# Attention of a two-layer gated network on one core: bank rotation, order of the query and key preparation, and two steps moved to GpSimd

## The chip, the cores and the metric

One Trainium2 chip, one of its cores. The metric is the device time of one execution in microseconds (us), lower is better. Names of engines: PE is TensorE, DVE is VectorE, ACT is ScalarE, POOL is GpSimd, SP is SyncE.

## The reference

Sixteen sequences ("batches") of 256 rows by 256 features go through four residual steps. Two of them matter here only as neighbours.

```
x += tanh(g_xattn[0]) * retention(layernorm(x), ctx)       # layer 0, decayed running sum
x += tanh(g_ffn[0])   * fp4_swiglu(layernorm(x))           # layer 0, 4-bit block quantised
x += tanh(g_xattn[1]) * attention(layernorm(x), ctx, ctx)  # layer 1, 16 heads of 16
x += tanh(g_ffn[1])   * bfp_mlp(layernorm(x))              # layer 1, block floating point
# attention: q = rope(q), k = rope(k); softmax(q k^T / 4 + alibi bias) v
```

All of it is float32 to the outside. x and ctx stay in SBUF from the first load to the last store.

## The kernel before, in words

The program of each engine is written out by hand; engines meet at counting semaphores. There are three stages over the 16 batches: layer 0, attention, and the MLP, and each engine's program runs a body per batch in each stage, with some work of neighbouring batches in it. The attention stage is the one that changes.

**Preparation of a batch (two bodies ahead).** DVE takes the layer-norm statistics of x (`at_qk_a`, L1477 to L1483), POOL raises the variance to the power -1/2 (`at_rstd`, L1178), DVE normalises (`at_qk_norm`, L1489 and L1492), POOL multiplies with the cosine and the sine table (`at_k_parts` L1173 and L1174, `at_q_parts` L1183 and L1184), DVE adds the two products (`at_rope`, L1501) and writes a rounded high part twice into a stack (`at_high_part`, L1513), POOL writes the rest as a low part (`at_low_part`, L1166). The stack holds q and k of all heads with bias rows, so that a product of two rounded matrices gives full precision.

**A body b of PE (`at_body`).** It transposes the stack of batch b+1 in eight groups of four (`at_turn`, L579), each into a 512-wide bank, and ACT copies each to SBUF (`at_turned`, L934). In between it transposes the row maxima of batch b (`at_turn_max`, L606), which ACT negates (`at_max_out`, L955) and SP places as two extra rows of the transposed stack with two DMAs (`at_place_max`, L398), and it transposes the output of batch b-1 (`at_turn_out`, L643). Then come, interleaved, sixteen groups m of score products of batch b+1 that serve only to find the row maxima (`at_scores_for_max`, L599; DVE reduces each with `at_row_max`, L1523), sixteen groups u of scores of batch b, already less their maximum (`at_scores`, L620; ACT takes the exponential of each, `at_exponent`, L943), and eight groups of products with the values (`at_times_v`, L635; ACT copies four results, `at_pv_out`, L949). Two groups u are issued among the transposes, and one after each m but 7 and 15.

**Banks.** PSUM has eight in the stage. Two (`a_ps_t`) take the transposed groups in turn, two (`a_ps_m`) take maxima groups, two the scores, two the values' product. From m = 4 on the maxima groups use `a_ps_t` and `a_ps_m` by pairs, so that four are in rotation; m = 2 and 3 reuse the banks of m = 0 and 1. The transposed maxima go into the first bank of `a_ps_m`.

**Body b of DVE:** statistics of b+2, rope and high part of k of b+2, norm of b+2, output of b-1 (`at_add_attention`: two reciprocals L1530, two products L1534, gate times result plus x at L1537), then the sixteen maxima of b+1, with rope of q after m = 5 and its high part after m = 8. **Body b of POOL:** k parts, rstd, low part of k, q parts, low part of q of b+2. ACT copies the values into a padded array after u = 8 (`at_v_of`, L926). Before the first body a prologue prepares the first two batches, interleaved with the end of layer 0, and finds the maxima of the first.

In the last but one body DVE and POOL round the MLP's weights, in the last PE transposes them.

Of the kernel before, what the change touches and what calls it, by code (L numbers as in the profile page):

```python
# [12 lines left out]
ALU = mybir.AluOpType  # L13
# [3 lines left out]
P = 128  # L17
# [107 lines left out]
V_QK = ["stats0", "stats1", "aggr0", "aggr1", "var", "rope_k", "k_hi", "rstd4", "norm0", "norm1", "rope_q", "q_hi"]  # L125
V_QK_FIRST = ["stats0", "stats1", "aggr0", "aggr1", "var", "rope_k", "rstd4", "norm0", "norm1", "k_hi", "rope_q", "q_hi"]
G_QK = ["k_cos", "k_sin", "rstd", "k_lo", "q_cos", "q_sin", "q_lo"]
G_QK_FIRST = ["k_cos", "k_sin", "rstd", "q_cos", "q_sin", "k_lo", "q_lo"]
V_OUT = ["recip0", "recip1", "share0", "share1", "add"]
# [14 lines left out]
LAST_IN_TURN_BANKS = 6  # L144


def build_main(nc, load, loaded, out_v, g_xattn, g_ffn, w_gate_up, w_down, w_fc, b_fc, w_proj, b_proj, ident, decay,
# [3 lines left out]
    with ExitStack() as keep:  # L151
# [146 lines left out]
        def group_in_same_max_bank(m):  # L298
            return m - 4 if m >= 6 else m - 2
# [44 lines left out]
        a_v_qk, a_g_qk, a_v_max, a_v_out = sem("v_qk"), sem("g_qk"), sem("v_max"), sem("a_v_out")  # L344
# [3 lines left out]
        a_alone = sem("a_waits_alone")  # L348
        f_v_ln, f_g_rstd, f_v_shift, f_a_norm = sem("f_v_ln"), sem("f_rstd_ready"), sem("f_shift_ready"), sem("f_normed")
# [13 lines left out]

        def v_qk_steps(b):
            return V_QK if b.shifted(-1) else V_QK_FIRST

        def g_qk_steps(b):
            return G_QK if b.shifted(-1) else G_QK_FIRST
# [57 lines left out]
        def _(pe):  # L426
# [220 lines left out]
            def at_body(b):  # L647
# [153 lines left out]
        def _(act):  # L801
# [119 lines left out]
            def at_v_of(b):  # L921
                if b.shifted(-2):
                    act.wait_ge(a_t_pv, b.shifted(-2).count(PG, PG))
                elif b.i == 0:
                    act.wait_ge(a_v_aug_laid, 1)
                nc.scalar.copy(a_v_aug[:, b.par, :, :, 0:HD].rearrange("p c h d -> p (c h) d"),  # L926
                               tiles(ctx, b).rearrange("p c (h d) -> p (c h) d", d=HD)).then_inc(a_v, 1)

            def at_turned(b, g):
                act.wait_ge(a_t_t, b.count(TG, g + 1))  # L930
                if g == 0 and b.shifted(-2):
# [3 lines left out]
                               a_ps_t[:, g % 2, :]).then_inc(a_t, 1)  # L935
# [21 lines left out]
            def at_body(b):  # L957
# [14 lines left out]
                for u in range(2, SU):  # L972
# [3 lines left out]
                    if u == 8 and nxt:  # L976
                        at_v_of(nxt)
# [80 lines left out]
            at_v_of(first)  # L1058
# [17 lines left out]
        def _(pool):  # L1076
# [84 lines left out]
            def at_low_part(b, which):  # L1161

                pool.wait_ge(a_v_qk, upto(v_qk_steps(b), b, ("q_hi", "k_hi")[which]))
# [3 lines left out]
                                        s[:, :, 0:HD], ALU.subtract).then_inc(a_g_qk, 1)  # L1167

            def at_k_parts(b):
# [3 lines left out]
                nc.gpsimd.tensor_tensor(a_part_cos[:, 1, :], kb, a_cos[:, :], ALU.mult).then_inc(a_g_qk, 1)  # L1173
                nc.gpsimd.tensor_tensor(a_part_sin[:, 1, :], kb, a_sin[:, :], ALU.mult).then_inc(a_g_qk, 1)  # L1174

            def at_rstd(b):
                pool.wait_ge(a_v_qk, upto(v_qk_steps(b), b, "var"))
                nc.gpsimd.tensor_tensor(a_rstd[:, b.par], a_var[:, b.par], neg_half[:, :], ALU.pow).then_inc(a_g_qk, 1)  # L1178

            def at_q_parts(b):  # L1180
                qb = a_qn[:, :, :].rearrange("p c d -> p (c d)")
                pool.wait_ge(a_v_qk, upto(v_qk_steps(b), b, "norm1"))
                nc.gpsimd.tensor_tensor(a_part_cos[:, 0, :], qb, a_cos[:, :], ALU.mult).then_inc(a_g_qk, 1)  # L1183
                nc.gpsimd.tensor_tensor(a_part_sin[:, 0, :], qb, a_sin[:, :], ALU.mult).then_inc(a_g_qk, 1)  # L1184
# [586 lines left out]
```

## Time and profile before

| what | value |
|---|---|
| median of 3 runs | 830.58 us (827.97 to 831.57) |
| profiled execution, its own time | 830.41 us |
| profiled execution, span | 828.3 us |
| PE, DVE, ACT, POOL busy over the span | 85%, 83%, 59%, 52% |
| attention bodies | from about 363 to 669 us |

The span runs from the first to the last instruction of the trace; the time of the execution holds 2.11 us more around it. In the timeline a row is: start in us, length in us, engine, line, operation, tiles, count, and in brackets how long the engine sat idle before it and what ended that. PEld is the weight load of a matmul. Rows merge neighbouring instructions; the ends of matmuls are modelled, so the distance between two starts tells more than a length.

### The profile page before, as it was taken

What the parts mean: (1) busy time and instruction counts of PE and PEld (TensorE: products, weight loads), DVE (VectorE), ACT (ScalarE), POOL (GpSimd) and SP (SyncE); (2) the same over time, 40 slices, a digit from 0 to 9 for tenths busy, and PEclk for the clock granted to TensorE, in tenths of its full rate; (3) what the DMA queues carried; (4) which work ended last, traced back from release to release, by engine and by line L of the source; (5) the groups of instructions that cost most, each with busy time, mean ns of one, the idle gap of its engine ahead of it and who ended that gap; (6) DMA issues with size and microseconds to landing.
All of it is one profiled execution on the core that took longest, in us unless ns stands there. A gap on an engine that the chain in (4) does not pass through costs nothing.

```text
span 828.3 us, 16569 instructions
## 1 busy us (share of the span) xinstructions
PE 706.1 (85%) x5090; PEld 516.6 (62%) x5090; DVE 689.9 (83%) x1230; ACT 485.8 (59%) x955; POOL 430.8 (52%) x331
## 2 busy tenths in 40 slices
PE   2365999999999998689999999999999867767775
PEld 1254888888888876566666666666665424444443
DVE  6856888888888788878999999899998558888885
ACT  3333445555445342338887788887887755555653
POOL 3523656555665655744445555544454426555553
PEclk9676999999999999889999999999999797898899
DMA  8710000000000000010000000000001000000011
GB/s 275 239 34 0 1 1 1 0 0 0 0 0 1 1 1 1 1 51 3 3 2 2 1 1 2 1 1 1 1 1 52 2 1 13 26 26 25 27 39 51
DMA packets 17719, 18.35 MB, mean 22 GB/s; under 512 B 1670, under 2 KB 16912, under 8 KB 17680
## 3 DMA queue, kind: packets, MB, share of 16 engines
q1 hardware_dynamic: 17084, 17.66, 6.6%
q8 instruction: 21, 0.34, 0.2%
q10 hardware_dynamic: 596, 0.20, 0.1%
q14 instruction: 18, 0.15, 0.1%
HBM read 13.39 MB, written 4.19 MB: 21 GB/s over the span
## 4 chain that ended last, share of the span: by engine, by line
PE 58%; DVE 18%; issue 9%; ACT 8%; POOL 4%; DMA 1%; POOLq 0%; DVEq 0%; ACTq 0%; SPq 0%
PE ps_o L540 9%; PE a_ps_pv L635 7%; PE a_ps_t L579 7%; PE a_ps_s L620 6%; PE a_ps_m L599 5%; DVE f_ps_small L1608 4%; PE ps_gu L504 4%; PE ps_gu L506 4%; PE ps_gu L505 4%; PE a_ps_t L599 3%; DVE f_hcode L1624 2%; DVE maxima L1523 2%; PE a_ps_pv L643 1%; ACT stack_t L934 1%; ACT probs L943 1%
## 5 line engine op out<-in xcount | busy, mean ns | idle before, releaser
L943 ACT ACTIVATE probs<-a_ps_s 128x512 f32<-128x512 f32 x256 | 148.1, 602 | 30.3 <-PE a_ps_s L620 25.7
L1523 DVE TENSOR_REDUCE maxima<-a_ps_m 128x2 f32<-128x512 f32 x160 | 102.6, 682 | 11.1 <-PE a_ps_m L599 11.0
L620 PE MATMUL a_ps_s<-stack_t 64*128 64x256 f32 x512 | 102.6, 315 | 3.1 <-ACT probs L943 1.5
L540 PE MATMUL ps_o<-w2t,hqt 128*128 128x256 f32 (+1 forms) x384 | 99.1, 393 | 1.3 <-ACT hqt L871 0.7
L1166 POOL TENSOR_TENSOR stack<-roped,stack 128x512 f32<-128x512 f32 x32 | 42.8, 1337 | 109.6 <-DVE stack L1513 108.2
L504 PE MATMUL ps_gu<-w1h,yth 128*128 128x352 f32 x256 | 86.8, 339 | 4.6 <-DVE h L1336 4.6
L934 ACT CAST stack_t<-a_ps_t 128x512 fp32r<-128x512 f32 x128 | 71.8, 584 | 31.1 <-PE a_ps_t L579 30.8
L635 PE MATMUL a_ps_pv<-probs,v_aug 128*32 128x256 f32 x1024 | 84.9, 404 | 3.0 <-ACT probs L943 2.9
L579 PE MATMUL a_ps_t<-idf,stack 128*128 128x128 f32 x512 | 76.8, 290 | 8.8 <-POOL stack L1166 5.1
L505 PE MATMUL ps_gu<-w1l,yth 128*128 128x352 f32 x256 | 83.1, 325 | 0.0
L506 PE MATMUL ps_gu<-w1h,ytl 128*128 128x352 f32 x256 | 83.1, 324 | 0.0
L540 PEld LDWEIGHTS ps_o<-w2t,hqt 128*128 128x128 f32 (+1 forms) x384 | 66.3, 189 | 22.1 <-issue 12.4
L620 PEld LDWEIGHTS a_ps_s<-stack_t 64*128 64x128 f32 x512 | 68.2, 191 | 16.4 <-ACT probs L943 8.9
L579 PEld LDWEIGHTS a_ps_t<-idf,stack 128*128 128x128 f32 x512 | 57.8, 146 | 25.6 <-ACT stack_t L934 8.8
L1523 DVE TENSOR_REDUCE maxima<-a_ps_t 128x2 f32<-128x512 f32 x96 | 62.9, 681 | 11.2 <-PE a_ps_t L599 11.2
L1140 POOL TENSOR_TENSOR hq<-hcode,hscale 128x1408 f32<-128x1408 bf16 x16 | 41.5, 2592 | 56.5 <-DVE hcode L1355 56.5
L599 PE MATMUL a_ps_m<-stack_t 64*128 64x256 f32 x320 | 66.1, 322 | 3.8 <-DVE maxima L1523 2.9
L863 ACT ACTIVATE sg<-ps_gu 128x352 f32<-128x352 f32 x64 | 29.6, 463 | 67.5 <-PE ps_gu L506 67.5
L599 PEld LDWEIGHTS a_ps_m<-stack_t 64*128 64x128 f32 x320 | 43.1, 187 | 34.3 <-DVE maxima L1523 18.8
L1215 POOL TENSOR_TENSOR f_hup<-f_h,f_hmag 128x2048 f32<-128x2048 f32 x16 | 58.3, 3641 | 10.5 <-DVE f_hcode L1624 9.5
L1005 ACT ACTIVATE f_h<-f_ps_fc 128x512 f32<-128x512 f32 x64 | 36.1, 597 | 36.4 <-POOL f_hup L1215 36.2
L1336 DVE TENSOR_TENSOR h<-sg,ps_gu 128x352 f32<-128x352 f32 x64 | 33.2, 518 | 28.2 <-ACT sg L863 27.9
(181 smaller groups left out, 1703.9 us busy)
## 6 DMA issues: line engine op xcount, KB each, us to landing
xres<-in_x SPq DMA_DIRECT2D x16, 256.0 KB, 3.2
ctx<-in_ctx SPq DMA_DIRECT2D x16, 256.0 KB, 3.8
out_x<-f_y SPq DMA_DIRECT2D x16, 256.0 KB, 2.1
w1a_raw<-in_w_gate_up SPq DMA_DIRECT2D x1, 1024.0 KB, 5.8
w_raw<-in_w_fc SPq DMA_DIRECT2D x1, 1024.0 KB, 5.5
w_raw<-in_w_proj SPq DMA_DIRECT2D x1, 1024.0 KB, 4.9
w_raw<-in_w_down SPq DMA_DIRECT2D x1, 704.0 KB, 9.2
stack_t<-neg_max_t SPq DMA_DIRECT2D x32, 8.0 KB
```

What stands on the lines that cost most here:

```text
L504: nc.tensor.matmul(into, yth[:, kc, c, :], w1h[:, kc, cols], start=kc == 0, stop=False)
L505: nc.tensor.matmul(into, yth[:, kc, c, :], w1l[:, kc, cols], start=False, stop=False)
L506: ins = nc.tensor.matmul(into, ytl[:, kc, c, :], w1h[:, kc, cols], start=False, stop=kc == KD - 1)
L540: ins = nc.tensor.matmul(ps_o[:, c, :], hqt[0:rows, g, n, :], w2t[0:rows, k, :], start=k == 0, stop=k == KH0 - 1)
L579: ins = nc.tensor.transpose(a_ps_t[:, g % 2, (n * C + c) * P:(n * C + c + 1) * P], a_stack[:, b.par, which, c, 2 * pair:2 * pair + 2, :].r ...
L599: ins = nc.tensor.matmul(max_bank(m)[:, n, :], a_stack_t[b.par][rows, 0, pair, c * P:(c + 1) * P], a_stack_t[b.par][rows, 1, pair, :], sta ...
L620: ins = nc.tensor.matmul(a_ps_s[:, half, n, :], a_stack_t[b.par][rows, 1, pair, kc * P:(kc + 1) * P], a_stack_t[b.par][rows, 0, pair, :], ...
L635: ins = nc.tensor.matmul(a_ps_pv[32 * n:32 * n + 32, quad % 2, 0:T], a_v_aug[:, b.par, kc, 4 * quad + n, :], a_probs[:, (2 * g + n % 2) % ...
L934: nc.scalar.copy(a_stack_t[b.par][:, g % 2, pair:pair + 2, :].rearrange("p a t -> p (a t)"), a_ps_t[:, g % 2, :]).then_inc(a_t, 1)
L943: nc.scalar.activation(a_probs[:, u % 8], a_ps_s[:, u % 2], ACT.Exp).then_inc(a_exp, 1)
L1215: nc.gpsimd.tensor_tensor(f_blocks(f_hup[:, :]), f_blocks(f_h[:, b.par]), f_spread(f_hmag[:, b.par], F_NBH), ALU.add).then_inc(f_g_hup, 1)
L1523: nc.vector.tensor_reduce(a_maxima[:, b.par, c, 4 * quad + half:4 * quad + half + 3:2], max_bank(m), X, ALU.max).then_inc(a_v_max, 1)
```

## The change

Transposed groups g and maxima groups m both rotate over the four banks of `a_ps_t` and `a_ps_m`, by pairs. Scores u follow every m up to 13. Statistics of batch b+4 and the norm of b+3 are taken in body b, rope and high parts of k and q of b+2 at its start, and nothing but maxima after m = 0. POOL multiplies the values by the attention gate (ACT copied them before), and POOL adds the attention's result to x. The one preparation counter of each engine becomes several. The MLP's statistics wait for POOL's addition. Core of the diff:

```diff
+        def turned_bank(g):
+            return (a_ps_t[:, g % 2, :], a_ps_m[:, g % 2].rearrange("p a t -> p (a t)"))[g // 2 % 2]
         def max_bank(m):
-            pair, half = m // 2, m % 2
-            if pair >= 2 and pair % 2 == 0:
-                return a_ps_t[:, half, :].rearrange("p (a t) -> p a t", t=T)
-            return a_ps_m[:, half]
+            return (a_ps_t[:, m % 2, :].rearrange("p (a t) -> p a t", t=T), a_ps_m[:, m % 2])[m // 2 % 2]
# PE, at_turn(b, g)
-                if g >= 2:
-                    pe.wait_ge(a_t, b.count(TG, g - 1))
+                if g >= 4:
+                    pe.wait_ge(a_t, b.count(TG, g - 3))
+                elif b.shifted(-1) and g >= 2:
+                    pe.wait_ge(a_mt, b.shifted(-1).count(1, 1))
                 elif b.shifted(-1):
-                    pe.wait_ge(a_v_max, b.shifted(-1).count(MU, 2 * LAST_IN_TURN_BANKS + g + 1))
+                    pe.wait_ge(a_v_max, b.shifted(-1).count(MU, MU - 3 + g))
# PE, at_scores_for_max(b, m)
-                if m == 0 and b.shifted(-1):
-                    pe.wait_ge(a_mt, b.shifted(-1).count(1, 1))
-                if m in (4, 5):
-                    pe.wait_ge(a_t, b.count(TG, TG + m - 5))
-                elif m >= 2:
-                    pe.wait_ge(a_v_max, b.count(MU, group_in_same_max_bank(m) + 1))
-                elif b.shifted(-1):
-                    pe.wait_ge(a_v_max, b.shifted(-1).count(MU, MU + m - 1))
+                if m >= 4:
+                    pe.wait_ge(a_v_max, b.count(MU, m - 3))
+                else:
+                    pe.wait_ge(a_t, b.count(TG, TG - 3 + m))
# PE, at_body
-                    if m % 8 != 7:
+                    if m < SU - 2:
# ACT: at_v_of and both its calls go; POOL:
+            def at_v_of(b):
+                if b.shifted(-2):
+                    pool.wait_ge(a_t_pv, b.shifted(-2).count(PG, PG))
+                    pool.sem_inc(a_alone, 1)
+                nc.gpsimd.tensor_tensor(a_v_aug[:, b.par, :, :, 0:HD]..., tiles(ctx, b)...,
+                                        gates[:, 1:2].unsqueeze(2).to_broadcast([P, C * NH, HD]), ALU.mult).then_inc(a_v, 1)
+            def at_add(b):
+                pool.wait_ge(a_v_out, upto(V_OUT, b, "share1"))
+                nc.gpsimd.tensor_tensor(tiles(xres, b), tiles(xres, b), a_attn[:, :, :], ALU.add).then_inc(a_g_add, 1)
             def at_body(b):
-                    at_k_parts(nxt2)
-                    at_rstd(nxt2)
                     at_low_part(nxt2, 1)
-                    at_q_parts(nxt2)
                     at_low_part(nxt2, 0)
-                elif b.shifted(1):
+                if nxt3:
+                    at_q_parts(nxt3)
+                if b.shifted(-1):
+                    at_add(b.shifted(-1))
+                if nxt4:
+                    at_rstd(nxt4)
+                if nxt3:
+                    at_k_parts(nxt3)
+                if b.shifted(1):
+                    at_v_of(b.shifted(1))
+                if b.shifted(1) and not nxt2:
                     w34_round(0)
                     w34_round(1)
# DVE, at_body (at_share is at_add_attention without its last instruction)
-                    at_qk_a(nxt2)
                     at_rope(nxt2, 1)
                     at_high_part(nxt2, 1)
-                    at_qk_norm(nxt2)
                 if b.shifted(-1):
-                    at_add_attention(b.shifted(-1))
+                    at_share(b.shifted(-1))
+                if nxt2:
+                    at_rope(nxt2, 0)
+                    at_high_part(nxt2, 0)
+                if nxt4:
+                    at_qk_a(nxt4)
+                if nxt3:
+                    at_qk_norm(nxt3)
...
-                    if nxt2 and m == 5:
-                        at_rope(nxt2, 0)
-                    if nxt2 and m == 8:
-                        at_high_part(nxt2, 0)
# DVE, prologue: among the maxima of the first batch
+                if m == 3:
+                    at_rope(second, 1)
+                    at_high_part(second, 1)
                 if m == 5:
                     l0_add_ffn(last)
                     at_rope(second, 0)
-                if m == 8:
                     at_high_part(second, 0)
+                if m == 9:
+                    at_qk_a(third)
+                if m == 12:
+                    at_qk_norm(third)
+                if m == 14:
+                    at_qk_a(fourth)
```

POOL's prologue ends with rstd, k parts and q parts of the third batch, rstd of the fourth and the values of the first. After the bodies, POOL adds the last batch's attention between two of the MLP's input steps.

## Rows read from the trace of the kernel before

**Rows 1.** The page, busy time of each engine over the span

```profile
PE 706.1 (85%) x5090; PEld 516.6 (62%) x5090; DVE 689.9 (83%) x1230; ACT 485.8 (59%) x955; POOL 430.8 (52%) x331
```

**Rows 2.** Busy time by stretch: two attention bodies; us, engines, granted clock, DMA

```profile
512.00:549.00 37.00, 35.84 (x344) 23.98 (x348) 33.84 (x67) 29.79 (x60) 18.84 (x15) 1.00 0.00 1
```

**Rows 3.** PE's timeline, the transpose of the maxima, four of its sixteen

```profile
364.57 0.64 PE L606 MATMUL a_ps_m<-idf,maxima 128*16 128x128 f32 x2
...
384.01 0.38 PE L606 MATMUL a_ps_m<-idf,maxima 128*16 128x128 f32 x2
...
532.05 0.38 PE L606 MATMUL a_ps_m<-idf,maxima 128*16 128x128 f32 x2
...
624.42 0.38 PE L606 MATMUL a_ps_m<-idf,maxima 128*16 128x128 f32 x2
```

**Rows 4.** PE's timeline through one body, 531 to 550 us

```profile
531.12 1.09 PE L579 MATMUL a_ps_t<-idf,stack 128*128 128x128 f32 x8
...
534.42 1.14 PE L579 MATMUL a_ps_t<-idf,stack 128*128 128x128 f32 x8 [0.24 <-ACT stack_t L934]
535.51 0.50 PE L620 MATMUL a_ps_s<-stack_t 64*128 64x256 f32 x2
...
537.54 0.52 PE L599 MATMUL a_ps_m<-stack_t 64*128 64x256 f32 x4
...
540.17 0.64 PE L635 MATMUL a_ps_pv<-probs,v_aug 128*32 128x256 f32 x8
...
541.42 0.64 PE L635 MATMUL a_ps_pv<-probs,v_aug 128*32 128x256 f32 x8
...
549.50 1.09 PE L579 MATMUL a_ps_t<-idf,stack 128*128 128x128 f32 x8
```

**Rows 5.** DVE's timeline through the same body

```profile
531.23 0.74 DVE L1477 BATCH_NORM_STATS2 a_stats<-xres 128x6 f32 x2
...
532.43 0.69 DVE L1501 TENSOR_TENSOR roped<-part_cos,part_sin 128x512 f32<-128x512 f32 x1
533.25 0.69 DVE L1513 CAST stack<-roped 128x1024 fp32r<-128x1024 f32 x1
...
534.22 1.57 DVE L1492 TENSOR_SCALAR qn<-xres,a_mv,a_rstd 128x256 f32 x2
535.71 0.36 DVE L1530 RECIPROCAL denom<-a_ps_pv 128x16 f32<-128x16 f32 x2
...
536.91 0.77 DVE L1537 SCALAR_TENSOR_TENSOR xres<-attn,gates,xres 128x512 f32 x1 [0.17 <-DVE attn L1534]
538.16 2.57 DVE L1523 TENSOR_REDUCE maxima<-a_ps_m 128x2 f32<-128x512 f32 x4 [0.48 <-PE a_ps_m L599]
541.27 1.29 DVE L1523 TENSOR_REDUCE maxima<-a_ps_t 128x2 f32<-128x512 f32 x2 [0.54 <-PE a_ps_t L599]
```

**Rows 6.** ACT's timeline through the same body

```profile
532.47 0.38 ACT L955 ACTIVATE neg_max_t<-a_ps_m 16x256 fp32r<-16x256 f32 x1
...
538.31 1.09 ACT L943 ACTIVATE probs<-a_ps_s 128x512 f32<-128x512 f32 x2
...
542.00 0.37 ACT L949 COPY pv_t<-a_ps_pv 128x256 f32<-128x256 f32 x1
```

**Rows 7.** POOL's timeline through the same body

```profile
532.58 1.40 POOL L1178 TENSOR_TENSOR a_rstd<-a_var,neg_half 128x2 f32<-128x2 f32 x1 [1.63 <-DVE a_var L1483]
534.02 1.29 POOL L1166 TENSOR_TENSOR stack<-roped,stack 128x512 f32<-128x512 f32 x1
...
537.10 1.73 POOL L1184 TENSOR_TENSOR part_sin<-qn,sin 128x512 f32<-128x512 f32 x1
```

**Rows 8.** Line L1492, lengths of one in ns, minimum, median and maximum

```profile
L1492 DVE TENSOR_SCALAR qn<-xres,a_mv,a_rstd x32: 399/411/1386, 325.1 to 609.4; 128x256 f32 x24, 128x256 f32<-128x256 f32 x8
```

**Rows 9.** ACT's and PE's timelines at the start of the last body

```profile
644.98 0.37 ACT L955 ACTIVATE neg_max_t<-a_ps_m 16x256 fp32r<-16x256 f32 x1 [0.20 <-PE a_ps_m L606]
...
648.04 0.50 PE L620 MATMUL a_ps_s<-stack_t 64*128 64x256 f32 x4 [0.68 <-DMA stack_t<-neg_max_t]
```

More of the change, by code:

```diff
@@ L124 @@
 V_ROUND = ["up", "codes"]
[L125 to L129, printed above, removed]
+V_STATS = ["stats0", "stats1", "aggr0", "aggr1", "var"]
+V_NORM = ["rstd4", "norm0", "norm1"]
+V_ROPE = ["rope_k", "k_hi", "rope_q", "q_hi"]
+G_LOW = ["k_lo", "q_lo"]
+V_OUT = ["recip0", "recip1", "share0", "share1"]
 V_IN1 = ["amax", "pow2", "magic"]
@@ L137 @@
 L0_BEHIND = 4
+ATT_AHEAD = 4
 FFN_AHEAD = 6
@@ L362, in build_main @@
         lead = [Batch(n // 2, n % 2) for n in range(FFN_AHEAD)]
[L364 to L368, printed above, removed]
         def upto_w(name):
@@ L919, in l0_body @@
                 l0_hidden_magic(b)
[L921 to L927, printed above, removed]
             def at_turned(b, g):
@@ L975, in at_body @@
                         at_pv_out(b, (u - 6) // 4)
-                    if u == 8 and nxt:
-                        at_v_of(nxt)
                     if not nxt and u == 9:
@@ L1056, in _ @@
             over_batches(act, l0_body, L0_AHEAD, L0_BEHIND)
-            at_v_of(first)
             for g in range(TG):
@@ L1161, in at_low_part @@
             def at_low_part(b, which):
-                pool.wait_ge(a_v_qk, upto(v_qk_steps(b), b, ("q_hi", "k_hi")[which]))
+                pool.wait_ge(a_v_rope, upto(V_ROPE, b, ("q_hi", "k_hi")[which]))
                 lo = (HD, R_HI2)[which]
@@ L1172, in at_k_parts @@
                     pool.wait_ge(a_tables, 48)
-                nc.gpsimd.tensor_tensor(a_part_cos[:, 1, :], kb, a_cos[:, :], ALU.mult).then_inc(a_g_qk, 1)
-                nc.gpsimd.tensor_tensor(a_part_sin[:, 1, :], kb, a_sin[:, :], ALU.mult).then_inc(a_g_qk, 1)
+                else:
+                    pool.wait_ge(a_v_rope, upto(V_ROPE, b.shifted(-1), "rope_k"))
+                nc.gpsimd.tensor_tensor(a_part_cos[:, 1, :], kb, a_cos[:, :], ALU.mult).then_inc(a_g_k, 1)
+                nc.gpsimd.tensor_tensor(a_part_sin[:, 1, :], kb, a_sin[:, :], ALU.mult).then_inc(a_g_k, 1)
@@ L1183, in at_q_parts @@
-                nc.gpsimd.tensor_tensor(a_part_cos[:, 0, :], qb, a_cos[:, :], ALU.mult).then_inc(a_g_qk, 1)
-                nc.gpsimd.tensor_tensor(a_part_sin[:, 0, :], qb, a_sin[:, :], ALU.mult).then_inc(a_g_qk, 1)
+                pool.wait_ge(a_v_norm, upto(V_NORM, b, "norm1"))
+                if b.shifted(-1):
+                    pool.wait_ge(a_v_rope, upto(V_ROPE, b.shifted(-1), "rope_q"))
+                nc.gpsimd.tensor_tensor(a_part_cos[:, 0, :], qb, a_cos[:, :], ALU.mult).then_inc(a_g_q, 1)
@@ L1252, in _ @@
             l0_hidden_quantised(last)
+            at_rstd(second)
             at_k_parts(second)
-            at_rstd(second)
+            at_q_parts(second)
             at_low_part(second, 1)
-            at_q_parts(second)
             at_low_part(second, 0)
-            over_batches(pool, at_body)
+            at_rstd(third)
+            at_k_parts(third)
+            at_q_parts(third)
+            at_rstd(fourth)
+            at_v_of(first)
+            over_batches(pool, at_body, ATT_AHEAD)
             for b in lead[:3]:
@@ L1264, in _ @@
             ff_input_up(lead[1])
+            at_add(last)
             ff_input_rstd(lead[4])
@@ L1498, in at_rope @@
             def at_rope(b, which):
-                dve.wait_ge(a_g_qk, upto(g_qk_steps(b), b, ("q_sin", "k_sin")[which]))
+                dve.wait_ge((a_g_q, a_g_k)[which], b.count(2, 2))
+                if b.shifted(-1):
+                    dve.wait_ge(a_g_low, upto(G_LOW, b.shifted(-1), ("q_lo", "k_lo")[which]))
                 nc.vector.tensor_tensor(at_halves(a_roped, which), at_halves(a_part_cos, which), at_halves(a_part_sin, which)[:, :, ::-1, :],
-                                        ALU.add).then_inc(a_v_qk, 1)
+                                        ALU.add).then_inc(a_v_rope, 1)
             def at_high_part(b, which):
                 step = (R_HI2, HD)[which]
-                dve.wait_ge(a_v_qk, upto(v_qk_steps(b), b, ("rope_q", "rope_k")[which]))
+                dve.wait_ge(a_v_rope, upto(V_ROPE, b, ("rope_q", "rope_k")[which]))
                 if b.shifted(-2):
@@ L1524, in at_row_max, with at_share @@
                                         ALU.max).then_inc(a_v_max, 1)
-            def at_add_attention(b):
+            def at_share(b):
                 for c in range(C):
@@ L1530, in at_add_attention @@
                     nc.vector.reciprocal(a_denom[:, c, :], bank[:, :, HD]).then_inc(a_v_out, 1)
+                if b.shifted(-1):
+                    dve.wait_ge(a_g_add, b.shifted(-1).count(1, 1))
                 for c in range(C):
@@ L1690, in _ @@
             at_qk_a(second)
-            at_rope(second, 1)
-            at_high_part(second, 1)
             at_qk_norm(second)
@@ L1717, in _ @@
             ff_input_shift(lead[3])
-            at_add_attention(last)
+            at_share(last)
             ff_input_magic(lead[2])
```

61 lines of the change are left out of this document (32 added, 29 removed).

## The prediction

> **What bounds the kernel now.** I read the page first, then the busy time by stretch, the chain of waits, and the timelines of PE, DVE, ACT and POOL through one attention body. The page puts PE at 85% and DVE at 83% of the span [rows 1]: two engines share the load, and neither average says what ends a body. The stretch of two bodies has PE at 35.84 and DVE at 33.84 of 37.00 us, ACT at 29.79, POOL at 18.84, and PE's granted clock at 1.00, its upper level [rows 2]. So ACT and POOL have room; PE and DVE have little, unless they wait for each other.
>
> The transposes of the maxima mark the bodies: from 384.01 to 624.42 us there are thirteen of them, 240.41 us, so a body takes 18.49 us [rows 3]. PE's timeline splits one of them, 531.12 to 549.50, at three places [rows 4]. (a) First transposes to first scores, 531.12 to 535.51: 4.39 us. (b) Scores and transposes in turn, to the first maxima group at 537.54: 2.03 us. (c) The rest, 11.96 us, with 16 maxima groups, 14 score groups and 8 value groups.
>
> Part (c) has the slack. Between the value groups at 540.17 and 541.42 lie two maxima, two score groups and one value group without a wait: 1.25 us. Seven such pairs are 8.75 us. A value group is 0.6 of it (0.64 long [rows 4]), so the four score and maxima groups are some 0.65. Two maxima groups more, 0.65 by that as an upper end, and the last value group, 0.6, make 10.0. So (c) contains about 1.9 us of waiting. DVE shows why. Its maxima begin at 538.16, 0.62 after PE issued the first group, take 0.60 each, and DVE sits idle 0.48 before the first and 0.54 before the fifth [rows 5]: groups 2 and 3 wait for the banks of 0 and 1, so PE cannot run ahead. Later, rope and the high part of q stand among the maxima, 0.6 to 0.8 us each [rows 5], and PE waits for them through the banks.
>
> **The change, part by part.**
>
> *Maxima over four banks from the first, nothing among them, scores after m = 7 too.* This takes the waits out of (c), down to PE's own 10.0, if ACT follows. ACT starts its exponentials at 538.31, 0.77 after the part begins, and a pair takes 1.09 with at most 0.37 for a copy of the value product after every second [rows 6]. Seven pairs and three copies are 8.7, so the last exponential ends 9.5 us in, or about 10 with two or three handovers of 0.2 over the two score banks. The last value group, which waits for it, ends 0.6 later. I take 10.5 for (c); the ends are 10.0 (no handover lost) and 10.9 (only DVE's two idle times of 0.48 and 0.54 vanish from 11.96).
>
> *Transposed groups over four banks.* The wait of 0.24 for ACT's copy at 534.42 [rows 4] goes, 0.4 with PE's refill. It is worth nothing: the first scores need the maxima placed by the two DMAs. ACT ends the negation at 532.85 [rows 6] and the scores start 2.66 later [rows 4]. In the last body nothing else stands in the way, PE is idle on the DMA for 0.68, and the distance is 648.04 less 645.35, 2.69 us [rows 9]. So (a) stays 4.39, and the DMA is late next. The new wait of groups 2 and 3 for the negation costs nothing: it ends 0.80 after 532.05 [rows 3, 6], while the output's eight transposes follow those of the maxima, and eight transposes take 0.93 (531.12 to 532.05). Part (b) stays 2.03. Sum: 4.39 + 2.03 + 10.5 = 16.9 us a body.
>
> *DVE.* Its stretch between maxima ran from 531.23 to 537.68, 6.45 us [rows 5]. The addition leaves it (0.77 and the wait of 0.17); rope and high part of q come in: 0.82 and 0.76 with their gaps [rows 5]. The order matters for a second reason. The two norm instructions took 1.57 while POOL's low part ran [rows 5, 7]; the median of one is 0.411 with the longest 1.386 [rows 8], so two take 0.8 and 0.7 was waiting. Likewise POOL's 1.73 for the sine product overlaps DVE's addition, against 1.29 for the low part [rows 7]. In the new order: rope and high part of k 1.6; reciprocals and shares 1.1 (535.71 to 536.8); rope of q, which begins while POOL writes the low part of k and waits some 0.3; its high part, together 1.8; statistics 1.2; norm 1.0, behind POOL's low part of q. That is about 6.6, and with sixteen maxima at 0.60 DVE's cycle is 16.2 us: under PE's 16.9, so it decides nothing, by 0.7 us. From the first maxima group PE gives DVE 16.9 less 9.6 and 0.6, 6.7 us: just enough.
>
> The Trainium skill's page "SBUF — State Buffer", section "Who interferes with whom", says that a VectorE instruction in a two-port mode or with two SBUF inputs and a GpSimd instruction exclude each other for a whole instruction. This trace agrees (0.4 alone, up to 1.386 beside POOL). By a full exclusion rope of q would wait 0.3 and no more, as in my sum; without any, DVE's cycle would be 15.9 and the body would still be PE's.
>
> *POOL.* Six products or differences of 1.29 (two low parts, two and two parts) stay; the values' product and the addition come in. Neither shape is in the trace; I take 1.29, the nearest row, and 1.73 as the upper end [rows 7]. With a power of 1.40 that makes 8 times 1.29 and 1.40, 11.7 us, or 12.6. It starts at DVE's first high part (1.6 in), stands until the norm (6.6), then has the q parts, addition, power, k parts and values, 9.2 us: done 15.8 in, 1.1 before the next body, so it is hidden. Were this cover gone, each further late instruction would cost DVE up to 1.3. ACT loses its copy of the values, hidden either way. The wait of values' product for the previous use of its array is long met. The MLP's wait for the addition is also met, since those batches were added bodies ago; POOL's last addition, 1.29, sits in front of a power that waits for DVE anyway.
>
> *Ends of the stage.* In the prologue three pieces (statistics twice, norm once: 3.4 us) are put between the first batch's maxima. Earlier maxima of groups 0 to 3 give back some 1, and POOL's products can hold the norm for up to 1.3. The first turn of the maxima, 364.57 [rows 3], moves to 367 or 368. The first body had two longer bank waits and gets back some 1.5. Net cost 2 us, between 0 and 4. The last but one body is DVE's, with weight rounding among the maxima; it loses the bank waits and the addition, 1.7. The tail loses one addition, 0.7.
>
> **The sum.** Thirteen bodies at 18.49 less 16.9 give 20.7. Time: 830.4 - 20.7 + 2.0 - 1.7 - 0.7 = 809.3, say 809. The profiled execution's 830.41 is the median within 0.2, so the sum holds for both.
>
> **The rivals.** *Handovers cost nothing* (A): (c) is 10.0, a body 16.4, thirteen save 27.2, time 803. For it: 1.25 us pairs exist, some with a copy in them. Against: ACT has 9.5 us of 10. *Only the visible bank waits go* (B): (c) 10.9, or DVE's stretch gets one more blocked instruction of 1.3 and its cycle becomes 17.5. A body takes 17.3 to 17.5 and the time is 813 to 817. For it: three engines now meet within 0.7 us, and a two-bank ring between ACT and PE lost time in the trace too. *The change does not remove what it names* (D): the maxima are held by something other than banks and rope; the time stays within 0.5%, 826 to 835. Against: DVE's idle times name PE, and the group after them waits for exactly that bank.
>
> *Slower* (C): DVE and POOL block each other. Six DVE instructions in the new stretch (two ropes, two high parts, two norms) can wait for a POOL instruction of 1.29, and POOL now works two thirds of a body. DVE's cycle is 16.2, so the change loses once these waits pass 2.3 us a body: two of them. Three make 20.0 us a body, thirteen lose 20, and the time is about 850. It needs POOL to run past the body's end; the 1.1 us left speak against it, POOL's 1.73 for them. A clock below the upper level would act on this side too, but the stretch with 97% of PE busy had 1.00 [rows 2].
>
> **How the numbers follow.** Mine 0.46, A 0.22, B 0.24, D 0.04, C 0.04. The likeliest gives 809; its own range is 805 to 813 by (c) and by the prologue. Down to A's 803 less 1 and up to B's 817 with 2 of the prologue's doubt, 802 to 819, leaves out D and C and a little of A. About 0.5% is what a measurement tells from no change here: faster by over 0.5% has 0.92, within 0.5% 0.04, slower 0.04.
>
> **What would show it.** The transposes of the maxima should stand 16.9 us apart; DVE should have no idle time before the fifth maxima group; the first scores should be idle on the DMA in most bodies, some 0.4 to 0.6; the last value group should wait for an exponential. Norm should take 0.8 for two. The addition and values' product should show on POOL near 1.3 with POOL idle before the next low part of k. I am wrong in mechanism if a body is bound by DVE's stretch, if POOL's timeline has no gap at the body's end, or if the value groups stand 1.5 apart with no wait for DVE.

## The result, and the profile after

The changed kernel takes 839.16 us (median of four runs, 837.54 to 840.83), the one before 830.08 beside it: a ratio of 1.0106 [1.0086 to 1.0126]. It is 1.1% slower, where 809 us was forecast with a range of 802 to 819.

The page, and the stretch of two bodies that answers to [rows 2] (PE, PEld, DVE, ACT, POOL busy, granted clock, DMA share, GB/s):

```profile
span 835.7 us, 16572 instructions
...
PE 699.1 (84%) x5090; PEld 512.5 (61%) x5090; DVE 680.5 (81%) x1214; ACT 478.2 (57%) x939; POOL 451.2 (54%) x363
...
512.00:549.00 37.00, 34.31 (x344) 22.84 (x337) 31.59 (x65) 28.64 (x58) 20.59 (x19) 1.00 0.00 1
```

PE fell from 35.84 to 34.31 of 37 us and DVE from 33.84 to 31.59 [rows 2], at the same clock. Neither engine became the bound: both wait more, and only POOL works more. The transposes of the maxima, which were 18.49 us apart [rows 3], now stand so:

```profile
388.25 0.38 PE L597 MATMUL a_ps_m<-idf,maxima 128*16 128x128 f32 x2
...
631.00 0.38 PE L597 MATMUL a_ps_m<-idf,maxima 128*16 128x128 f32 x2
```

That is 242.75 us over thirteen bodies, 18.67 each. One of them in PE's timeline, to hold against [rows 4]:

```profile
541.41 0.50 PE L611 MATMUL a_ps_s<-stack_t 64*128 64x256 f32 x2 [0.52 <-DMA stack_t<-neg_max_t]
...
543.44 0.52 PE L590 MATMUL a_ps_t<-stack_t 64*128 64x256 f32 x4
...
544.12 0.64 PE L626 MATMUL a_ps_pv<-probs,v_aug 128*32 128x256 f32 x8
...
549.54 0.51 PE L590 MATMUL a_ps_t<-stack_t 64*128 64x256 f32 x4
549.88 0.40 PE L611 MATMUL a_ps_s<-stack_t 64*128 64x256 f32 x4
550.21 0.64 PE L626 MATMUL a_ps_pv<-probs,v_aug 128*32 128x256 f32 x8
550.78 0.65 PE L590 MATMUL a_ps_m<-stack_t 64*128 64x256 f32 x3
...
551.73 0.50 PE L611 MATMUL a_ps_s<-stack_t 64*128 64x256 f32 x2 [0.18 <-ACT probs L926]
552.16 0.64 PE L626 MATMUL a_ps_pv<-probs,v_aug 128*32 128x256 f32 x8
552.73 0.51 PE L590 MATMUL a_ps_t<-stack_t 64*128 64x256 f32 x4
553.07 0.41 PE L611 MATMUL a_ps_s<-stack_t 64*128 64x256 f32 x4
553.40 0.64 PE L626 MATMUL a_ps_pv<-probs,v_aug 128*32 128x256 f32 x8
...
554.91 0.64 PE L626 MATMUL a_ps_pv<-probs,v_aug 128*32 128x256 f32 x8 [0.44 <-ACT probs L926]
555.50 1.09 PE L574 MATMUL a_ps_t<-idf,stack 128*128 128x128 f32 x8
```

Scores to first maxima group is 541.41 to 543.44, part (b) with its 2.03. Part (c) is 543.44 to 555.50, 12.06 where 10.5 was forecast. From 548.97 on the value groups stand 1.24 and 1.95 apart in turn (before that 1.66, 1.33 and 1.86): two pairs take 3.19 us instead of 2.5. ACT and DVE in the same body:

```profile
550.31 0.60 ACT L926 ACTIVATE probs<-a_ps_s 128x512 f32<-128x512 f32 x1 [0.64 <-PE a_ps_s L611]
550.80 0.37 ACT L932 COPY pv_t<-a_ps_pv 128x256 f32<-128x256 f32 x1
551.05 1.81 ACT L926 ACTIVATE probs<-a_ps_s 128x512 f32<-128x512 f32 x3
553.50 0.60 ACT L926 ACTIVATE probs<-a_ps_s 128x512 f32<-128x512 f32 x1 [0.63 <-PE a_ps_s L611]
```

```profile
542.86 0.74 DVE L1502 TENSOR_SCALAR qn<-xres,a_mv,a_rstd 128x256 f32 x2
544.08 1.29 DVE L1534 TENSOR_REDUCE maxima<-a_ps_t 128x2 f32<-128x512 f32 x2 [0.48 <-PE a_ps_t L590]
...
550.08 1.29 DVE L1534 TENSOR_REDUCE maxima<-a_ps_t 128x2 f32<-128x512 f32 x2 [0.57 <-PE a_ps_t L590]
...
553.26 1.29 DVE L1534 TENSOR_REDUCE maxima<-a_ps_t 128x2 f32<-128x512 f32 x2 [0.65 <-PE a_ps_t L590]
```

ACT waits for PE once in four exponentials, and PE waits for ACT, 0.18 at a time: these two stand in a ring. DVE waits for PE before every fourth maxima, because PE's maxima groups are queued behind the waiting scores.

**The ring, step by step**, with the starts of single instructions in this body; u counts the score groups from 0. Scores use two banks, so group u waits for exponential u-2. Scores 10 start at 549.88, and their exponential starts 0.43 later. The next exponential could follow 0.49 after that, but ACT's program has the copy of a value product in between: 0.25 more. Exponential 11 then takes 0.60. PE, standing at scores 13 for its bank, starts them 0.07 later. Behind them in PE's queue are a value group (issued 0.44 later), two maxima groups (0.57 later) and scores 14 (0.34 later), at 553.07. Sum: 0.43 + 0.49 + 0.25 + 0.60 + 0.07 + 0.44 + 0.57 + 0.34 = 3.19 us for four score groups, which is 553.07 less 549.88. The links follow on each other without a gap, so they must add up to that distance; what they show is who holds whom. PE's own work in it is 2.5 at the forecast's 1.25 a pair, ACT's is four times 0.49 and 0.25, 2.2. Neither engine's own work fills the 3.19; the sum of the links is what counts.

A score group that waits costs twice: its wait, and its partner. The even and the odd groups read different halves of the rows, and when both are ready, four maxima matmuls or four score matmuls take 0.33 to 0.34 (549.54, 549.88, 550.21); the delayed group's two take 0.43 alone (551.73 to 552.16).

POOL did what was said of it:

```profile
546.24 1.28 POOL L1180 TENSOR_TENSOR xres<-xres,attn 128x512 f32 x1
547.47 0.71 POOL L1168 TENSOR_TENSOR a_rstd<-a_var,neg_half 128x2 f32<-128x2 f32 x1
...
550.62 1.04 POOL L1162 TENSOR_TENSOR v_aug<-ctx,gates 128x512 f32<-128x512 f32 x1
557.30 1.29 POOL L1146 TENSOR_TENSOR stack<-roped,stack 128x512 f32<-128x512 f32 x1 [5.64 <-DVE stack L1524]
```

**The ledger of the 7.4 us of span** (835.7 less 828.3): the attention stage begins 1.1 later, after layer 0, whose code did not change; the prologue is 2.1 longer, the first body 1.0, thirteen bodies 2.3; the last but one is 0.6 shorter; what follows it is 1.4 longer.

The prologue's part of it is work of DVE. A stretch of the kernel after, and then of the one before (columns as above):

```profile
358.00:371.00 13.00, 8.83 (x32) 6.65 (x33) 12.69 (x26) 2.16 (x5) 9.38 (x9) 0.50 0.01 1
```

```profile
358.00:371.00 13.00, 11.38 (x54) 8.54 (x54) 10.61 (x22) 5.71 (x10) 8.50 (x7) 0.74 0.21 63
```

DVE is busy for 12.69 of the 13 us, against 10.61 before. PE, which waits for it, shows this:

```profile
357.99 1.36 PE L590 MATMUL a_ps_m<-stack_t 64*128 64x256 f32 x4 [2.39 <-DVE maxima L1534]
...
367.79 0.60 PE L597 MATMUL a_ps_m<-idf,maxima 128*16 128x128 f32 x2 [1.47 <-DVE maxima L1534]
```

And DVE, the last of the statistics and the last maxima group:

```profile
365.67 0.74 DVE L1486 BATCH_NORM_STATS2 a_stats<-xres 128x6 f32<-128x256 f32 x2
...
367.05 0.68 DVE L1534 TENSOR_REDUCE maxima<-a_ps_m 128x2 f32<-128x512 f32 x1
```

From 355.17 on DVE's instructions follow each other without a wait, and PE's transpose of the maxima starts 0.06 after the last of them ends. The three pieces put among the maxima take 4.5 us there (359.56 to 360.74, 362.54 to 364.47, 365.67 to 367.05). PE's clock is at its lower level, 0.50 (1.2 GHz), for all of those 13 us, but PE has time to spare in them. The clock costs something only behind 367.79: the first scores start 4.23 us later, where it was 3.72 before, so some 0.5 of the 1.0 that the first body lost. Eight transposes take 1.76 there from start to start (368.85 to 370.61), and 0.88 at the upper level (538.98 to 539.86).

### The profile page after: what moved, and what is told of

Read it like the earlier page. It is cut to its first block, busy times and chain, and to the rows that moved or that the text cites. A ratio compares the mean times of both kernels' runs of the same rounds, so it can differ in the third digit from the quotient of the medians.

```text
span 835.7 us, 16572 instructions
## 1 busy us (share of the span) xinstructions
PE 699.1 (84%) x5090; PEld 512.5 (61%) x5090; DVE 680.5 (81%) x1214; ACT 478.2 (57%) x939; POOL 451.2 (54%) x363
## 4 chain that ended last, share of the span: by engine, by line
PE 50%; DVE 17%; issue 11%; ACT 10%; DMA 6%; POOL 4%; SPq 2%; ACTq 1%; POOLq 0%; DVEq 0%
PE ps_o L533 9%; PE a_ps_s L611 6%; PE a_ps_pv L626 5%; DVE f_ps_small L1620 4%; PE ps_gu L497 4%; PE ps_gu L499 4%; PE ps_gu L498 4%; DMA stack_t<-neg_max_t 3%; PE a_ps_t L590 3%; ACT probs L926 3%; PE a_ps_m L574 3%; DMA ctx<-in_ctx 2%; PE a_ps_t L574 2%; DVE f_hcode L1636 2%; ACT pv_t L932 2%
## 5 line engine op out<-in xcount | busy, mean ns | idle before, releaser
L1534 DVE TENSOR_REDUCE maxima<-a_ps_t 128x2 f32<-128x512 f32 x128 | 82.7, 686 | 34.0 <-PE a_ps_t L590 34.0
L611 PE MATMUL a_ps_s<-stack_t 64*128 64x256 f32 x512 | 88.5, 302 | 16.3 <-DMA stack_t<-neg_max_t 8.8
L1534 DVE TENSOR_REDUCE maxima<-a_ps_m 128x2 f32<-128x512 f32 x128 | 82.4, 685 | 1.6 <-PE a_ps_m L590 1.4
L611 PEld LDWEIGHTS a_ps_s<-stack_t 64*128 64x128 f32 x512 | 61.1, 188 | 35.8 <-ACT probs L926 18.9
L1218 POOL TENSOR_TENSOR f_hup<-f_h,f_hmag 128x2048 f32<-128x2048 f32 x16 | 58.2, 3640 | 10.5 <-DVE f_hcode L1636 9.5
L497 PEld LDWEIGHTS ps_gu<-w1h,yth 128*128 128x128 f32 x256 | 48.8, 191 | 7.7 <-DVE h L1345 6.5
L715 PE MATMUL f_ps_h<-idb,f_hcode 128*128 128x128 bf16 x256 | 24.9, 254 | 33.8 <-DVE f_hcode L1636 33.7
L1114 POOL TENSOR_TENSOR hs<-h,hrinv 128x1408 f32<-128x1408 f32 x16 | 42.7, 2666 | 13.8 <-DVE hrinv L1315 13.8
L590 PEld LDWEIGHTS a_ps_m<-stack_t 64*128 64x128 f32 x256 | 31.9, 189 | 28.9 <-DVE maxima L1534 14.8
L498 PEld LDWEIGHTS ps_gu<-w1l,yth 128*128 128x128 f32 x256 | 48.8, 191 | 0.4
```

The costliest lines, as they stand in the source:

```text
L497: nc.tensor.matmul(into, yth[:, kc, c, :], w1h[:, kc, cols], start=kc == 0, stop=False)
L498: nc.tensor.matmul(into, yth[:, kc, c, :], w1l[:, kc, cols], start=False, stop=False)
L590: ins = nc.tensor.matmul(max_bank(m)[:, n, :], a_stack_t[b.par][rows, 0, pair, c * P:(c + 1) * P], a_stack_t[b.par][rows, 1, pair, :], sta ...
L611: ins = nc.tensor.matmul(a_ps_s[:, half, n, :], a_stack_t[b.par][rows, 1, pair, kc * P:(kc + 1) * P], a_stack_t[b.par][rows, 0, pair, :], ...
L1114: nc.gpsimd.tensor_tensor(blocks(hs[:, :]), blocks(h[:, :]), spread(hrinv[:, b.par], NBH), ALU.mult).then_inc(g_hs, 1)
L1218: nc.gpsimd.tensor_tensor(f_blocks(f_hup[:, :]), f_blocks(f_h[:, b.par]), f_spread(f_hmag[:, b.par], F_NBH), ALU.add).then_inc(f_g_hup, 1)
```

## The experiments

Each ratio is to the kernel before run beside that kernel, whose median was 830.08 to 830.91. The theory: (1) the ring of two score banks holds part (c). Rivals: the value group's place in PE's order; the scores packed without a gap (they now follow m = 7); the work moved to POOL; the prologue. "Body" is the mean of the thirteen.

| kernel | score banks | maxima banks | body | part (c) | median | ratio to before |
|---|---|---|---|---|---|---|
| before | 2 | 2, later 4 | 18.49 | 12.00 | 830.08 | 1 |
| after | 2 | 4 | 18.67 | 12.12 | 839.16 | 1.0106 [1.0086, 1.0126] |
| a_copy | 2 | 4 | 17.84 | 11.30 | 826.59 | 0.9948 [0.9930, 0.9966] |
| b_copy | 2 | 2, later 4 | 18.16 | 11.67 | 823.23 | 0.9899 [0.9859, 0.9939] |
| b_banks | 2 | 4 | 18.26 | 11.74 | 825.20 | 0.9927 [0.9900, 0.9955] |
| b_banks_copy | 2 | 4 | 17.97 | 11.45 | 820.85 | 0.9885 [0.9849, 0.9921] |
| a_order | 2 | 4 | 18.28 | 11.74 | 832.15 | 1.0020 [0.9997, 1.0043] |
| a_tv | 2 | 4 | 18.34 | 11.79 | 837.23 | 1.0085 [1.0059, 1.0112] |
| a_copy_tv | 2 | 4 | 18.90 | 12.33 | 845.59 | 1.0174 [1.0150, 1.0197] |
| a_pro | 2 | 4 | 18.77 | 12.21 | 836.69 | 1.0069 [1.0048, 1.0090] |
| a_all | 2 | 4 | 18.88 | 12.33 | 843.50 | 1.0159 [1.0137, 1.0181] |
| a_three | 3 | 3 | 17.42 | 10.91 | 822.33 | 0.9915 [0.9889, 0.9942] |
| b_three_copy | 3 | 3 | 17.45 | 10.96 | 820.03 | 0.9877 [0.9849, 0.9906] |
| a_three_copy_pro | 3 | 3 | 16.83 | 10.30 | 807.99 | 0.9723 [0.9684, 0.9761] |

**a_copy and b_copy: one link of the ring.** ACT's copy of a value product moves behind the odd exponential, in the kernel after and in the one before.

```diff
-                    if u % 4 == 2 and u >= 6:
-                        at_pv_out(b, (u - 6) // 4)
+                    if u % 4 == 3 and u >= 7:
+                        at_pv_out(b, (u - 7) // 4)
```

> The changed kernel with one move on ScalarE: each copy of the values' product (L932) stands after the odd exponential of its pair and no longer between the even and the odd one. Theory 1, the ring: scores have two banks, the odd score group waits for the odd exponential two groups back, and the copy between the two delays it, so that every second pair takes 1.9 us in place of 1.25; with the copy moved all pairs take 1.25 to 1.35, a body 16.9 to 17.3 us and the kernel 814 to 821 us. Theory 2, PE's own order or its handovers with DVE set the pace: a body stays at 18.6 and the time at 836 to 842.

> The kernel before with the same move of the copies and nothing else. Theory 1: its bank waits for DVE stay, so only what the ring cost beside them goes: a body 17.8 to 18.3 us, 820 to 828 us. Theory 2: no change, 829 to 832 us.

A move that removes no work takes 0.83 us from a body of the one and 0.33 from a body of the other, so the ring already ran in the kernel before. The gain in a_copy is about half of what I expected, the one in b_copy is inside its range. ACT and PE in a_copy:

```profile
538.91 1.09 ACT L926 ACTIVATE probs<-a_ps_s 128x512 f32<-128x512 f32 x2 [0.50 <-PE a_ps_s L611]
539.89 0.38 ACT L932 COPY pv_t<-a_ps_pv 128x256 f32<-128x256 f32 x1
540.23 1.09 ACT L926 ACTIVATE probs<-a_ps_s 128x512 f32<-128x512 f32 x2
```

```profile
537.57 0.64 PE L626 MATMUL a_ps_pv<-probs,v_aug 128*32 128x256 f32 x8
...
538.89 0.64 PE L626 MATMUL a_ps_pv<-probs,v_aug 128*32 128x256 f32 x8
...
540.48 0.64 PE L626 MATMUL a_ps_pv<-probs,v_aug 128*32 128x256 f32 x8
```

Two pairs now take 2.91 us, 540.48 less 537.57. The links without the copy's 0.25 add up to 2.94. The copy left the ring, and the ring stayed.

**b_banks and a_order: the rotation alone, and the packing.** b_banks is the kernel before with the four-bank rotation of turned and maxima groups and nothing else. a_order is the kernel after with the old gap in the scores, `if m % 8 != 7:` for `if m < SU - 2:`.

> The kernel before with the rotation over four banks alone (transposed groups and maxima groups); order of scores, preparation, values and addition as before. Theory 1: the waits for the banks of groups 2 and 3 go, but the ring of the scores takes their place: 825 to 832 us, no change that can be told. Theory 2 (banks set the pace before): 1 us a body, 813 to 820 us.

> The changed kernel with PE's old order of the score groups (none after maxima groups 7 and 15). Theory 1: the ring sets the pace whichever slots the groups stand in: within 3 us of the changed kernel, 836 to 842 us. Theory 3, closing the gap at group 7 put the copies where they hurt: back to 18.2 us a body or less, 832 to 835 us.

The rotation alone gives 0.23 us a body, so the waits for banks that I had seen were real and small. In b_banks' trace it also shortens the prologue, from 25.95 to 24.07 us. Packing the scores costs 0.39 a body, 5 us of the result: the gap at m = 7 had given the ring room. Theory 1 as I had written it, any slot is as good, missed by 4 us; theory 3 had it. With the old gap the kernel after has b_banks' body, 18.28 to 18.26. The new order on DVE and the steps given to POOL are worth nothing a body while two banks hold the scores. Outside the bodies they cost: the two medians are 7 us apart, and in the traces a_order's prologue is 4.6 longer than b_banks', its first body 1.0, its last but one 0.7.

**a_tv and a_copy_tv: what PE does while it waits.** The value group follows the even score group; a_copy_tv has the copy's move too.

```diff
-                        if u % 2 == 0 and u >= 4:
-                            at_times_v(b, (u - 4) // 2)
+                        if u % 2 == 1 and u >= 5:
+                            at_times_v(b, (u - 5) // 2)
+                    elif m == SU - 2:
+                        at_times_v(b, PG - 2)
```

> The changed kernel with PE's value group issued after the even score group of a pair, no longer after the odd one. Theory 1a: the odd score group waits for the odd exponential two groups back, and the value group and the next maxima stand behind it on PE, so each wait is paid by the whole engine (0.43 + 0.5 + 0.6 + 0.04 + 0.43 + 0.57 + 0.34 = 2.91 us for two pairs with the copy elsewhere, 3.18 with it between). With the value group ahead of the waiting one it covers the wait: a body 17.2 to 17.8 us, 820 to 828 us. Rival: the loop is ScalarE's own time plus the way from PE and back, wherever PE's work stands: a body 18.4 to 18.7, 836 to 841 us.

> Both: the copy after the odd exponential and the value group after the even score group. Theory 1a: pairs of 1.25 to 1.35 us, a body 16.7 to 17.2, 811 to 818 us; if DVE's cycle (6.4 of preparation, 9.6 of maxima, 0.6 for the first group, 16.6) comes next, not under 16.6. Rival: as with the copy alone, 17.8 a body and 825 to 828 us.

In a_tv two pairs take 2.91 as in a_copy, but with the value group gone from before the fifth score group PE idles 0.45 there, once a body; in a_copy_tv, which I took for the better of the two, they take 3.19 again. The scores now pair up odd with even, so the copy at its old place falls behind the pair, and at the new one into it. What counts is whether the copy stands between two exponentials that the ring needs in a row. Independent work put in front of the wait does not help: it is a link as well. That a value group could cover the wait, theory 1a, is refuted.

**a_pro: the prologue.** The third and the fourth batch's statistics and norm move from m = 9, 12 and 14 to just after m = 3 and 4, and POOL's two powers ahead of a low part.

> The changed kernel with the prologue's statistics and norm of the third batch and statistics of the fourth moved ahead, into the stretch in which DVE waits for the end of layer 0 (after maxima 3 and 4 of the first batch), and POOL's powers for them among its low parts. The prologue is 2.2 us longer than before by the time from the first transposes to the first turn of the maxima (28.10 for 25.95 us). If the inserted 3.4 us are the cause, 2 to 4 us go: 835 to 837.5 us. If it is the order of POOL or the clock, nothing: 838 to 841 us.

The prologue falls from 28.1 to 26.1 us, as it was before the change. The median falls by 2.5, but the two ratios' intervals touch, and the profiled execution of a_pro is no faster than that of the kernel after (837.9 us of span to 835.7), so only the prologue's gain is shown. The moved pieces fill time in which DVE had waited (0.31 and 1.00 in the kernel after), and the norm no longer runs beside POOL (0.73 instead of 1.64). DVE stays the bound of the stretch shown above, busy for 12.82 of 13 us, and the clock is now at 0.62:

```profile
358.00:371.00 13.00, 10.52 (x49) 8.26 (x49) 12.82 (x21) 4.40 (x8) 10.09 (x8) 0.62 0.10 26
```

**a_all: copy, value group and prologue together.**

> The three together. The savings stand in different stretches and should add: 16.7 to 17.2 us a body and the prologue's 2 to 4 us, 808 to 815 us, under both kernels. Rival: DVE or the DMA of the maxima sets the body once the ring is open, 17.5 a body and 818 to 824 us.

It repeats a_copy_tv's 18.9 a body and is 2.1 us faster, so the prologue's gain shows and no more.

**a_three: the ring with a third bank.** The eight banks are dealt anew: three for scores, three for turned and maxima groups. Two waits in the last body guard the new places.

```diff
-        a_ps_t = psum("a_ps_t", [P, 2, 512])
-        a_ps_m = psum("a_ps_m", [P, 2, 2, T])
-        a_ps_s = psum("a_ps_s", [P, 2, 2, T])
+        a_ps_x = psum("a_ps_x", [P, 3, 512])
+        a_ps_s = psum("a_ps_s", [P, 3, 2, T])
...
-                if u >= 2:
-                    pe.wait_ge(a_exp, b.count(SU, u - 1))
+                if u >= 3:
+                    pe.wait_ge(a_exp, b.count(SU, u - 2))
```

> The changed kernel with the banks dealt anew: three for the scores, three for transposed and maxima groups (two and four before). Theory 1b, from the runs so far: two banks bound the scores, whatever the order on PE; two pairs take 0.43 (scores to exponential) + 0.5 + 0.6 + 0.04 + 0.43 + 0.57 + 0.34 = 2.91 us at the least, and 3.18 with the copy between. A third bank lets PE run a group ahead, and part c falls from 12.1 to 10.2 to 10.8 us: a body 16.7 to 17.3, 812 to 821 us. Rival: DVE needs four banks for its maxima, or ScalarE's 0.54 and the handover set the pace alone: a body 18 or more, 828 to 840 us.

A body falls from 18.67 to 17.42, though the maxima have one bank less than the change gave them; so banks for the maxima are not what had held it. Body and time end just above my ranges.

**a_three_copy_pro: the third bank, the copy and the prologue.**

> The same with the copy after the odd exponential and the third and fourth batch's preparation early in the prologue. Theory 1b: with three banks the place of the copy matters little (within 0.3 us a body); the prologue gives 2 us. 808 to 818 us, the fastest so far. Rival as for the three banks alone, less 2 us.

```profile
528.02 0.64 PE L625 MATMUL a_ps_pv<-probs,v_aug 128*32 128x256 f32 x8
...
529.27 0.64 PE L625 MATMUL a_ps_pv<-probs,v_aug 128*32 128x256 f32 x8
...
531.84 0.64 PE L625 MATMUL a_ps_pv<-probs,v_aug 128*32 128x256 f32 x8
```

```profile
509.96 10.34 DVE L1535 TENSOR_REDUCE maxima<-a_ps_x 128x2 f32<-128x512 f32 x16
```

These value groups stand 1.25 to 1.30 apart, DVE takes sixteen maxima with no pause over 0.12 us, a body is 16.83 and the kernel 807.99 us. It is the fastest of all and beats both kernels.

**b_banks_copy and b_three_copy: is the rest of the change needed?** Both keep the kernel before's DVE order, values on ACT and addition on DVE. The first is b_banks with the copy moved; the second has the bank split of a_three, PE's packed order and the copy moved.

> The kernel before with the four-bank rotation and the copy's move, and nothing else of the change. Each alone gave 0.23 and 0.33 us a body. Theory 1b: DVE's waits and the copy's part of the ring go together, part c 11.1 to 11.4, a body 17.6 to 17.9, 815 to 821 us. Rival: they hide each other, 822 to 825 us.

> PE's program and the banks of the fastest kernel (three and three, scores after every maxima group to 13, copy after the odd exponential), with everything else as before the change: DVE's preparation in its old order with rope and high part of q among the maxima, addition on DVE, values on ScalarE, old prologue. If the part of the change that relieves DVE is worth something once the scores no longer bound the body: DVE's cycle is 6.45 of preparation, 1.2 among the maxima, 9.6 of maxima and 0.6 for the first group, 17.85 us, so a body 17.6 to 18.0 in place of 16.8, and 816 to 822 us. If the banks and the copy were all that mattered: 16.8 to 17.1 a body, 806 to 812 us.

b_banks_copy repeats the copy's gain, 0.29 a body. b_three_copy stops at 17.45. Four bodies of it, then DVE within one:

```profile
440.00:514.00 74.00, 71.79 (x720) 49.03 (x720) 71.42 (x142) 62.15 (x127) 40.99 (x31) 1.00 0.00 1
```

```profile
509.10 1.56 DVE L1487 TENSOR_SCALAR qn<-xres,a_mv,a_rstd 128x256 f32 x2
...
516.29 0.68 DVE L1496 TENSOR_TENSOR roped<-part_cos,part_sin 128x512 f32<-128x512 f32 x1
...
519.28 4.40 DVE L1518 TENSOR_REDUCE maxima<-a_ps_x 128x2 f32<-128x512 f32 x7
```

DVE is busy 71.42 of 74 us, and from 440 to 600 us it waits over 0.15 us for no other engine, only 1.9 us in all for results of its own. PE counts as busy for 71.79, so busy time alone would not tell them apart. With the ring open, DVE is the bound. Relieving it is worth 17.45 less 16.83, 0.62 us a body or 8 over thirteen. The change's other half is right for the bodies and had nothing to act on.

## Why the prediction was wrong, by its own steps

**(a) and (b): right.** (b) is 2.03 as forecast. (a) was to stay 4.39 with the first scores idle on the DMA, 0.4 to 0.6; it is 4.5, and the scores wait 0.51 to 0.62. The transposed groups' rotation is worth nothing there, as I said.

**(c): the step that failed.** "Seven pairs and three copies are 8.7, so the last exponential ends 9.5 us in, or about 10 with two or three handovers of 0.2 over the two score banks." It adds up ACT's work, and above it PE's, and takes the larger. In a ring with two banks the links of both engines add up instead: 3.19 us for four groups. The seven steps from the first value group to the last, 544.12 to 554.91, take 10.79 us against my 8.75: 2.0 more, of which I had allowed 0.5. The 1.25 us pair in [rows 4] misled me: it is the short half of the same alternation. Its neighbours in the kernel before:

```profile
538.22 0.64 PE L635 MATMUL a_ps_pv<-probs,v_aug 128*32 128x256 f32 x8
...
543.36 0.64 PE L635 MATMUL a_ps_pv<-probs,v_aug 128*32 128x256 f32 x8
```

The pair ahead of it took 1.95. The pair behind it took 1.94, with the copy at 542.00 [rows 6] in it, and from 540.17 to 543.36 two pairs take the ring's 3.19 already.

**The attribution before it failed as well.** "So (c) contains about 1.9 us of waiting. DVE shows why." DVE's idle time does name PE, but the waits of the kernel before (us in total, times, longest, over ten bodies) have a larger one between the other pair of engines, and I did not follow it:

```profile
ACT probs L943 <- PE a_ps_s L620: 15.5, 39, 0.7
...
DVE maxima L1523 <- PE a_ps_t L599: 5.4, 10, 0.6
DVE maxima L1523 <- PE a_ps_m L599: 5.3, 10, 0.7
```

In the kernel after, by the same view, ACT's wait is 25.3:

```profile
ACT probs L926 <- PE a_ps_s L611: 25.3, 55, 0.6
```

b_banks takes away the waits for banks and finds 0.23 us; a_order takes rope and high part of q out from among the maxima too and finds no more. The least that I allowed was 1.1 (11.96 to 10.9). b_copy, which touches neither banks nor rope, finds 0.33.

**A removed gap was costed at nothing.** The phrase "scores after m = 7 too" stands in the prediction among what takes the waits out of (c), and has no price; a_order shows that it costs 0.39 us a body.

**DVE: right, and without effect, as said.** Its stretch was forecast at 6.6 and is 6.4; two norms take 0.74 instead of 1.57 [rows 5], now that POOL is idle beside them. The Trainium skill's page "SBUF — State Buffer", section "Who interferes with whom", has a VectorE instruction in a two-port mode and a GpSimd instruction exclude each other for a whole instruction. The 0.74 without a POOL instruction beside it and, in b_three_copy, the 1.56 with one agree with it.

**POOL: right.** Addition 1.28 (forecast 1.29), values 1.04 (1.29), and the power 0.71 against 1.40 [rows 7]. It is idle 5.64 us before the next body's first low part; I left 1.1. Rival C, slower by DVE and POOL blocking each other, had the sign and not the cause.

**Ends: the prologue right, the rest not.** I said 2 for the pieces between the maxima and it is 2.1, by the mechanism that I gave. Both terms were too small: the pieces cost 4.5 and not 3.4, the norm among them 1.64 beside POOL, and the earlier maxima gave back more than "some 1" (1.9 in b_banks). That the errors cancel is luck. a_pro moves the same pieces and has the two us back. The first body, which "gets back some 1.5", lost 1.0; the last but one gained 0.6 of 1.7. The tail was to gain 0.7 and lost 1.4.

**Rival B named the ring** ("a two-bank ring between ACT and PE lost time in the trace too") and priced it as lost handovers, 0.4 to 0.6 us a body beyond mine. The arithmetic for the open ring holds for a body: a_three_copy_pro has 16.8 where 16.9 was forecast, and DVE is busy there for 71.17 of 74 us, 16.2 a body, as forecast. That its 808 also meets the 809 is partly luck, since in its trace the ends come out otherwise than in my sum (the stage begins 1.0 later, the prologue costs 0.7, the first body gives 0.9, the last but one costs 0.7). What failed was that this change does not open it.

## What to carry to other kernels

When two engines hand banks to each other, add the links of one round trip (matmul to reader, reader, every instruction queued between two readers, reader back to matmul, and what stands behind the waiting matmul in its queue, until the pattern repeats). Compare that with each engine's own work for the same groups, here 3.19 us for four groups with 2.5 and 2.2, before moving anything. If the round trip is larger, relieving the engines gives nothing (18.28 to 18.26 us here) and closing a gap in the order can cost; another bank, or one copy less between two readers, is what gives. Take a price such as 1.25 us over a whole period of the pattern, not from one step of it.

## What was not expected

The copy's place kept its worth with three banks: of the 0.59 us a body between a_three and a_three_copy_pro, the prologue's part touches no such body, and I had expected little from the copy there. Which link it stands in then was not taken apart.

The time behind the last regular body varies, and so does the clock there. From the last body's transposes of the maxima to its last output transpose the kernel before takes 24.7 us, after 26.7, a_copy 27.7. Stretches of a_copy, then of the kernel before:

```profile
650.00:662.00 12.00, 11.67 (x70) 6.22 (x70) 3.56 (x11) 8.82 (x17) 2.39 (x3) 0.50 0.00 1
```

```profile
650.00:662.00 12.00, 11.54 (x82) 5.95 (x85) 7.05 (x28) 10.10 (x20) 4.84 (x6) 0.58 0.01 2
```

PE counts as busy 97% at 0.50 in a_copy. Medians and bodies therefore don't line up. The clock isn't all of it: a_tv's body is 0.33 shorter than after's, 4.3 over thirteen, its time only 1.9, and from its last body on its trace is 3.5 us longer than after's, at the same mean clock, 0.86 and 0.85. Why was not taken apart, and nothing here says how to keep the clock up in the last body.

The wait of the first scores for the DMA, 0.4 to 0.6 in a regular body, is left in every kernel with the four-bank or the three-bank rotation; the kernel before and b_copy show none there. A single transfer for both rows was not tried.
